# Feature-major token loads, centred on GpSimd, in place of sixteen TensorE transposes per sequence

## What is computed

```
x = x + attn(layernorm(x))            # linear attention without softmax
x = x + xattn(layernorm(x), ctx)      # cross-attention with softmax
x = x + ffn(layernorm(x))             # shared MLP plus 16 routed experts, top 2

attn, s = 4 heads of h = 128, xn = layernorm(x) as (b, t, a, e):
  Q    = einsum('btae,aeqf->qbtaf', xn, queries)
  pre  = einsum('qbtaf,buqf->qbtau', Q, xn)
  mix  = einsum('qbtau,buqg->abtqg', pre, xn)
  out  = einsum('abtk,akg->btag', mix, combiners)
```

## Time and profile before

| | |
|---|---|
| median of 3 runs | 1875.05 us (1871.57 to 1876.61) |
| the profiled execution: its time | 1873.81 us |
| the profiled execution: its span | 1872.1 us |
| TensorE busy | 1848.3 us (99%), mean granted clock 0.996 |
| VectorE, ScalarE, GpSimd busy | 821.4, 759.4, 837.7 us |
| 16 transposes of YT, per sequence | 1.75 us on TensorE |
| one round of phase 1 (Q end to Q end) | about 63 us |

### The profile page before, as it was taken

One profiled execution on the slowest core, in us unless ns is written; L12 is line 12 of the kernel. 1 busy time (PEld: TensorE's weight loads), 2 busy tenths in 40 slices (PEclk: granted clock), 3 DMA queues, 4 the chain that ended last, 5 costly groups with the idle time before them and its releaser, 6 DMA issues.

```text
span 1872.1 us, 27265 instructions
## 1 busy us (share of the span) xinstructions
PE 1848.3 (99%) x10224; PEld 1629.4 (87%) x10224; DVE 821.4 (44%) x2007; ACT 759.4 (41%) x1492; POOL 837.7 (45%) x727
## 2 busy tenths in 40 slices
PE   8999999999999999999999999999999999999997
PEld 6788888888878787888799999999999999999996
DVE  2575557555764434344332344323444234443332
ACT  3444444444454333333443444434444334444331
POOL 2132333233462423222555665656656666556631
PEclk9999999999999999999999999999999999999999
DMA  7002220221164333221767666766666666666732
GB/s 269 21 12 79 91 91 1 91 91 68 69 180 57 46 45 78 40 43 16 158 155 152 137 146 130 163 151 143 143 128 162 152 145 143 130 153 157 145 46 28
DMA packets 208498, 199.18 MB, mean 106 GB/s; under 512 B 132944, under 2 KB 132944, under 8 KB 208112
## 3 DMA queue, kind: packets, MB, share of 16 engines
q1 hardware_dynamic: 183072, 144.34, 29.2%
q0 software_dynamic: 25296, 53.11, 16.8%
HBM read 119.14 MB, written 48.91 MB: 90 GB/s over the span
## 4 chain that ended last, share of the span: by engine, by line
PE 96%; DVE 1%; ACT 1%; issue 1%; another core or an unknown queue 0%; DMA 0%; POOL 0%; SPq 0%; ACTq 0%; DVEq 0%; POOLq 0%
PE ps L71 63%; PE ps L1389 23%; PE ps L747 4%; PE ps L753 2%; PE ps L885 2%; PE ps L844 1%; PE ps L764 1%; DVE buffer L1291 0%; DVE buffer L1307 0%; ACT L1247 0%; ACT buffer L1247 0%; DMA buffer<-in_WkT 0%; ACT buffer L1205 0%; PE ps L823 0%
## 5 line engine op out<-in xcount | busy, mean ns | idle before, releaser
L71 PE MATMUL ps<-buffer,buffer 128*128 128x320 f32 (+1 forms) x6816 | 1224.1, 340 | 3.4 <-DVE buffer L648 2.1
L71 PEld LDWEIGHTS ps<-buffer,buffer 128*128 128x128 f32 x6816 | 1105.2, 188 | 109.7 <-issue 3.3
L1147 POOL TENSOR_TENSOR buffer<-buffer,buffer 128x512 fp32r<-128x512 f32 x289 | 379.5, 1478 | 247.4 <-ACT buffer L1205 247.0
L1389 PE MATMUL ps<-buffer,buffer 128*128 128x512 f32 x1904 | 437.7, 390 | 1.4 <-DVE buffer L1291 1.4
L1389 PEld LDWEIGHTS ps<-buffer,buffer 128*128 128x128 f32 x1904 | 355.9, 188 | 76.0 <-issue 2.0
L1205 ACT ACTIVATE buffer<-buffer 128x512 fp32r<-128x512 f32 (+1 forms) x491 | 293.6, 651 | 163.0 <-PE ps L1389 90.9
L1247 ACT ACTIVATE buffer<-ps 128x320 f32<-128x320 f32 (+1 forms) x240 | 112.4, 468 | 589.9 <-PE ps L71 563.8
L1307 DVE TENSOR_TENSOR ps<-ps,buffer 128x320 f32<-128x320 f32 (+2 forms) x198 | 100.2, 506 | 489.7 <-ACT buffer L1247 481.9
L1194 POOL DMA_INDIRECT out_tokens<-buffer,slot_list x80 | 125.9, 1573 | 185.5 <-DVE buffer L1337 179.8
L387 POOL DMA_INDIRECT slots<-pairs,slot_u x64 | 63.4, 991 | 189.1 <-DVE slot_u L734 171.9
L395 ACT ACTIVATE buffer<-ps 128x512 fp32r<-128x512 f32 (+1 forms) x180 | 97.2, 602 | 100.7 <-PE ps L71 40.0
(11 more groups left out here) (112 smaller groups left out, 1088.3 us busy)
## 6 DMA issues: line engine op xcount, KB each, us to landing
buffer<-in_wts SPq DMA_DIRECT2D x289, 256.0 KB
buffer<-in_x SPq DMA_DIRECT2D x8, 1024.0 KB, 6.5
buffer<-in_ctxT SPq DMA_DIRECT2D x8, 1024.0 KB, 7.9
out_tokens<-buffer SPq DMA_DIRECT2D x8, 1024.0 KB, 4.3
tokens_normed<-buffer SPq DMA_DIRECT2D x32, 256.0 KB, 3.2
out_tokens<-buffer POOLq DMA_DIRECT2D x32, 256.0 KB, 5.7
tokens_normed<-buffer POOLq DMA_DIRECT2D x1, 1280.0 KB, 11.8
out_tokens<-buffer POOLq DMA_DIRECT2D x1, 1280.0 KB, 13.9
```

What stands on the lines that cost most here:

```text
L71: last = pe.matmul(out, left, right, start=(c == 0 and i == 0), stop=(c == len(parts) - 1 and i == 2))
L1147: pool.tensor_tensor(wl[n % RING][:], wraw[n % RAW][:], wh[n % RING][:].bitcast(F32), ALU.subtract).then_inc(s_wl, 1)
L1389: ins = pe.matmul(down_bank[n % 2][:], left, right, start=(c == 0 and i == 0), stop=(c == FC - 1 and i == len(passes) - 1))
```

## The change

The host also passes the tokens with features on partitions (`xT`), which SyncE loads into the place of `yT`. After the statistics, VectorE copies the four means of each partition to a tile `mean` (L566 of the new file); SyncE stores it to a 512-number row in DRAM and loads that row back into `mean_row` on all 128 partitions (new step MEAN); GpSimd subtracts it from the four 128x512 blocks of `xT` in place. So A gets centred but unscaled tokens, and VectorE multiplies by `rstd` when it adds A to the tokens. The 16 transposes of YT and their four ScalarE copies are gone. The first of the four groups of SC now follows G directly on TensorE, ahead of T. At the start, QB comes ahead of T, and MEAN between C and WV. The core of the diff:

```diff
+    xT = at(8, [NC, S])
+    mean_row = at(42, [S])
-    yT = at(8, [NC, S])
...
+        def load_transposed(b):
+            sp.dma_start(xT[:], a["xT"][b].rearrange("(c p) n -> p c n", p=P)).then_inc(s_xT, 16)
+
+        load_transposed(0)
...
+            if name == "MEAN":
+                sp.wait_ge(s_mean, b + 1)
+                with nc.allow_non_contiguous_dma(reason="one number per partition and tile"):
+                    sp.dma_start(means[b].rearrange("(t p) -> p t", p=P), mean[:]).then_inc(s_mstored, 16)
+                sp.wait_ge(s_mstored, 16 * (b + 1))
+                if b >= 1:
+                    sp.wait_ge(s_centred, NC * b)
+                sp.dma_start(mean_row[:], means[b].partition_broadcast(P)).then_inc(s_mrow, 16)
+            if name == "A" and b + 1 < B:
+                filled(sp, "A", b, NT - 1)
+                load_transposed(b + 1)
...
+            if name == "MEAN":
+                pool.wait_ge(s_xT, 16 * (b + 1))
+                pool.wait_ge(s_mrow, 16 * (b + 1))
+                for c in range(NC):
+                    pool.tensor_tensor(xT[:, c, :], xT[:, c, :], mean_row[:], ALU.subtract).then_inc(s_centred, 1)
...
-                for c in range(NC):
-                    filled(act, "YT", b, c)
-                    bank = bank_of("YT", b, c)
-                    copy(yT[:, c, :], bank[:]).then_inc(s_ev["YT"], 1)
...
+            if k == 0:
+                dve.wait_ge(s_mstored, 16 * b)
+                dve.tensor_copy(mean[:], mv[:, :, 0]).then_inc(s_mean, 1)
...
-                    dve.tensor_tensor(x[b % XS][:, t, :], bank[:], x[b % XS][:, t, :], ALU.add).then_inc(s_ev["A"], 1)
+                    dve.scalar_tensor_tensor(x[b % XS][:, t, :], bank[:], rstd[0][:, t:t + 1], x[b % XS][:, t, :],
+                                             ALU.mult, ALU.add).then_inc(s_ev["A"], 1)
...
-                drained(pe, "Q", b - 1, 1)
-                if b == 0:
-                    drained(pe, "KR", 0)
-                    drained(pe, "W", 0, NC - 1)
-                for c in range(NC):
-                    transposes("YT", b, y, c)
+                if b >= 1:
+                    drained(pe, "Q", b - 1, NC - 1)
+                    scores(b - 1, 0)
...
-                drained(pe, "YT", b, NC - 1)
+                pe.wait_ge(s_centred, NC * (b + 1))
...
-                        last = pe.matmul(bank_of("A", b, t)[:, cols], yT[:, h, t * P:(t + 1) * P], M[:, cols],
+                        last = pe.matmul(bank_of("A", b, t)[:, cols], xT[:, h, t * P:(t + 1) * P], M[:, cols],
...
-                 ("T", i + 1), ("WV", i + 1), ("QB", i + 1), ("SC", i), ("M", i + 1), ("PT", i),
+                 ("MEAN", i + 1), ("QB", i + 1), ("T", i + 1), ("WV", i + 1), ("SC", i), ("M", i + 1), ("PT", i),
...
+            steps.remove(("MEAN", 0))
+            steps.insert(steps.index(("WV", 0)), ("MEAN", 0))
```

More of the change, by code:

```diff
@@ L78, in build @@
     slots = nc.dram_tensor("slots", (E * CAP, 2), F32, kind="Internal").ap()
+    means = nc.dram_tensor("means", (B, S), F32, kind="Internal").ap()
     with ExitStack() as ctx:
@@ L94, in build @@
             "slots": slots,
+            "means": means,
             "ps": [ctx.enter_context(nc.psum_tensor(f"ps{i}", [P, 512], F32)) for i in range(BANKS)],
@@ L103, in phase1 @@
     ident, slot_list, slots = shared["ident"], shared["slot_list"], shared["slots"]
+    means = shared["means"]
     ps = shared["ps"]
@@ L207, in phase1 @@
     mv = sb("mv", [P, NT, 2], F32)
+    mean = sb("mean", [P, NT], F32)
     veps, rt = sb("veps", [P, NT], F32), sb("rt", [P, NT], F32)
@@ L247, in phase1 @@
     s_dve = sem("s_dve")
+    s_mean, s_mstored, s_mrow = sem("s_mean"), sem("s_mstored"), sem("s_mrow")
+    s_xT, s_centred = sem("s_xT"), sem("s_centred")
     s_cnt = sem("s_cnt")
@@ L757, in tensor, with scores @@
         pe.wait_ge(s_const, 8)
+        def scores(b, t):
+            cols = slice(t * P, (t + 1) * P)
+            ready = (lambda c: drained(pe, "Q", b, c)) if (b, t) == (B - 1, 0) else None
+            three_pass(pe, bank_of("SC", b, t)[:], [(qh[:, c, cols], ql[:, c, cols], ch[:, c, :], cl[:, c, :])
+                                                    for c in range(NC)], ready).then_inc(s_mm["SC"], 1)
         def step(name, b):
@@ L772, in step @@
             if name == "QB":
-                drained(pe, "YT", 0, 0)
                 bank = bank_of("QB", b)
@@ L840, in step @@
                     pe.wait_ge(s_w, 32)
+                    drained(pe, "KR", 0)
+                    drained(pe, "W", 0, NC - 1)
                 drained(pe, "Q", b - 1, 3)
@@ L846, in step @@
             if name == "SC":
-                if b < B - 1:
-                    drained(pe, "Q", b, NC - 1)
-                else:
+                if b == B - 1:
                     drained(pe, "V", b, 1)
-                drained(pe, "YT", b + 1, 3)
-                for t in range(NT):
-                    cols = slice(t * P, (t + 1) * P)
-                    ready = (lambda c: drained(pe, "Q", b, c)) if (b, t) == (B - 1, 0) else None
-                    three_pass(pe, bank_of("SC", b, t)[:], [(qh[:, c, cols], ql[:, c, cols], ch[:, c, :], cl[:, c, :])
-                                                            for c in range(NC)], ready).then_inc(s_mm["SC"], 1)
+                for t in range(1 if b < B - 1 else 0, NT):
+                    scores(b, t)
             if name == "X":
@@ L1426 @@
         "x": np.asarray(x),
+        "xT": np.ascontiguousarray(np.asarray(x).transpose(0, 2, 1)),
         "ctxT": np.ascontiguousarray(np.asarray(ctx_1024).transpose(0, 2, 1)),
```

2 lines of the change are left out of this document (1 added, 1 removed).

## The result

The change makes the kernel **slower**: 1938.17 us (median of 4 runs, 1936.91 to 1939.71) against 1873.93 us for the kernel before (now the median of 4 runs; the 1875.05 ahead of the prediction was that of the first 3), a ratio of 1.0343 with a 95% interval of [1.033, 1.0356]. The profiled execution took 1936.91 us, its span is 1935.2, 63.1 more than the 1872.1 before. I had forecast 1870.8, a small gain, with a range from 1866.5 to 1878. The measured time is outside the range, and the change is a loss.

What follows compares the result with a forecast made beforehand. TensorE, busy 99% of the span, was taken as the bound. Transposes -12.25, rounds' chain 0, start +5.5 and clock +2.5 sum to -4.25 us: 1870.8 us against the 1875.05 median, range 1866.5 to 1878.

Steps and rivals of the forecast that it cites:

- the transposes: TensorE in rounds 0 to 6: YT's transposes removed, 1.75 us each round, -12.25 us in all.
- the chain of the means in the rounds: Statistics, store, row load and subtractions ahead of A: ready at 222.5, wanted at 223.8, so a term of 0.
- the start: A of sequence 0 waits for GpSimd's subtractions behind C: 5.5 us later, at 50.05; bounds 5.0 and 8.3.
- the clock at the start: TensorE idles about 7 us before A of sequence 0, which then runs at low clock, once: 2.5 us, bounds 0 and 4.
- The store of 512 numbers lands right behind it; I give it 0.5.: SyncE's queue in a round: the means' store lands 0.5 us after the 1 MB token load ahead of it.
- The 1.3 us of slack: Ahead of A in a round: centred tokens ready 1.3 us before TensorE wants them.
- The means come late: Rival: the small-piece store pays its own landing of 5.7, A waits 3.9 in five rounds, 1890.3 us; chance 0.11.
- Much of 5.7 is GpSimd's own issue: Argument against the late-means rival: much of the earlier small-piece store's 5.7 us landing was GpSimd issuing it.
- 5.4 when it is alone: The 1 MB token load ahead of the means' store in a round: lands after 5.4 us, 7.3 at most.
- The row load "2.7": Load of the means' row, 256 KB, in a round: 2.7 us, taken from stores of halves at 2.1 to 3.3.
- The row is there by 44: At the start: the means' row is loaded by 44 us, before GpSimd's step C ends.
- The extras of 0.5: At the start: C beginning up to 0.9 later and disturbed GpSimd subtractions, taken as 0.5 us in all.

Runs made afterwards that it cites:

- experiment 1: Kernel of the change with the means stored as 128 pieces of 16 bytes, GpSimd reading the row in that order: 1896.95 us, ratio 1.0124.
- experiment 7: Kernel of the change, start only: context load and sequence 0's means ahead of token loads 1 and 2, means subtracted before the zeros wait: 1928.87 us.
- experiments 5: Kernel of the change without store, row load or subtraction of the means, centring left out: 1865.68 us, ratio 0.9961 to the kernel before.
- 6: Kernel of the change without any means, centring left out, and with QB back behind WV: 1859.47 us, ratio 0.9922 to the kernel before.
- experiment 3: Kernel of the change with the means' store for sequences 2 to 7 issued earlier, at the head of PV: 1885.72 us, ratio 1.0047.
- 12: Sequence 0 as in the kernel before; sequences 1 to 7 by early 16-byte means stores, row load ahead of token load: 1861.24 us, ratio 0.9927.
- experiment 11: Kernel before plus only VectorE's copy of the means and the four-byte store behind the token load, nobody waiting: 1874.34 us, ratio 0.9995.
- experiments 10: Three kernels on experiment 3, centring left out: four-byte pieces 64 bytes apart, 16 bytes apart, or a quarter as many: 1872.07, 1871.32, 1878.2 us.
- experiment 4: Kernel of the change loading 128 different token rows instead of the means' row, centring left out: 1933.86 us (one execution).
- experiment 9: Kernel of the change with rearranged start, early store, 16-byte pieces, row load ahead of token load: 1868.24 us; with QB back behind WV: 1867.27 us.

## Why the prediction was wrong

Term by term, forecast and measured: the transposes -12.25 and -12.25; the chain of the means in the rounds 0 and 48.8 of waits, with another 10.1 of A at the low clock behind them; the start 5.5 and 13.4; the clock at the start 2.5 and 2.3, with 1.6 more in V and Q.

- **The step that failed** is this one: "The store of 512 numbers lands right behind it; I give it 0.5." The store took 11.7 us from issue in round 2, 6.25 more than in my chain. Together with the row load (5.5 instead of 2.7, and 0.1 to issue it), subtractions 0.1 shorter, and the store issued 1.1 us later against TensorE than I had it, that makes 22.3 - 13.2 + 1.1 = 10.2 us. The 1.3 us of slack are taken off: 8.9 us, and 8.98 were measured. The term of 0 became 48.8. Round 6 is in it with 5.4 us: I had counted it out because no token load stands in the queue there, but the store took 9.0 all the same.
- **Its rival was there, in kind.** *The means come late* named the small pieces as the cause, and experiment 1 bears it out. But I costed its strong form at 5.7 us from the earlier trace rows, which is a store of other pieces (40 bytes each), and from there argued down. "Much of 5.7 is GpSimd's own issue" was a wrong reading: the trace of before has 1.18 us for that issue. The same means in another layout take 1.4 us, and in the first one 8.1 to 13.6 in the rounds of all kernels that have it. A price that was in no row deserved a wide bound and more than 0.11. The row that I put next to it against the rival, "stores of 256 KB land after 2.1", is one of large pieces and says nothing of small ones.
- **The token load "5.4 when it is alone"**: with the store behind it, it landed after 9.7 to 12.4 in three of five rounds and after 5.4 and 5.5 in the other two. The wait in A was there in all five (7.8 to 9.1), so this is not what it came from.
- **The row load "2.7"** was taken from stores of the same size. To read one row 128 times took 4.4 to 7.5 us in the kernel of the change. Even with a store that lands as forecast (experiment 1) waits of up to 3.3 us are left, of which the row load has 2.4.
- **The clock, "due here, once"**: right in kind and in size at the start (A 6.10 instead of 3.84, 2.3 us; I had 2.5). But after each of the waits in the rounds the clock was at 0.50 too. I had priced a late chain as a wait alone, and never as a wait plus 1.5 to 2.0 us of A at the low clock (5.27 to 5.74 in TensorE's timeline, where it is 3.74 before). The shorter waits of experiment 1 brought it as well: A took 5.44 to 6.56 behind four waits of 2.5 to 3.3 us, and 3.81 behind one of 1.8.
- **The start**: A(0) at 57.94 instead of 50.05. "The row is there by 44" failed: it was there at 52.7, since the store took 23.9 and the load 7.5. The layout is part of this: with 16-byte pieces (experiment 1) the same store takes 19.1 and A(0) starts at 52.25. Even with the means early (experiment 7), a wait of 4.3 stayed. What I hadn't seen is that QB ahead of T moves VectorE's subtractions into GpSimd's, for 6.2 us once the means are out of the way (experiments 5 and 6). The extras of 0.5 were counted on GpSimd, and the loss is mainly on VectorE. In the kernel of the change itself this cost nothing: the zeros landed so late that VectorE's four were done, in 2.50 us, before step C began.
- **Right**: the transposes are worth 1.75 us each (rounds of 61.26, experiment 3; a ratio of 0.9922 for eight in 6, which is 14.6 us; 12.7 to 13.7 for seven in 12). The score group behind G waits for nothing, the scaled drain of A and the later context load cost nothing. (5.4 after 214.8 is 220.2 and not the 220.6 that I wrote; nothing hangs on it.) Of what I wrote as signs of a wrong forecast, the wait in A several times over came in all six rounds; the token load landing after 7 us came in three of five and not in each.

## What to carry to other kernels

When a value has to go through DRAM to change its layout, the form of the store decides: keep a partition's numbers together, or the small pieces apart (64 bytes here), and issue it one stage before it is needed: the slow store that nobody waited for cost nothing (experiment 11). Count what the new layout costs its reader, here 1.1 us of strided subtractions. A transfer for which no row exists gets its bounds from pieces of its own size and layout, and a wait on the bound engine costs its own length and the slow matmuls behind it. Where a step is expensive only in one place (here the start), keep the old way there and take the new one elsewhere.

## What the runs showed of the hardware

- Four-byte pieces that lie close together in DRAM are slow: 1.9, 2.3 to 3.0 and 8.7 to 11.5 us for 512 of them in the rounds, with one, four and sixteen to 64 bytes (experiments 10 and 3); 7.5 to 8.1 for 128 of them side by side. 128 pieces of 16 bytes, side by side, take 1.4.
- With such a store behind it in the same queue, a load of 1 MB was reported as landed after 10.2 to 11.6 us in three of five rounds, and after 5.5 and 5.7 in the other two (experiment 11).
- A load of one 2 KB row to 128 partitions takes 5.8 us (median of the kernel of the change), 128 different rows 3.7 us (experiment 4).
- GpSimd's four 128x512 subtractions take 4.93 us, and 6.0 when one input is read with a stride of four numbers (experiment 1).
- VectorE instructions with two SBUF inputs beside GpSimd's: one took 11.2 us instead of 0.68, while GpSimd's own four went from 4.93 to 6.29 at most (experiment 7), and the strided four from 6.0 to 6.91 (experiment 9). The Trainium skill, GPSIMD Engine Reference, section Key points, says that GpSimd shares its SBUF interfaces with VectorE and contends with VectorE's instructions that have two SBUF inputs; the rows agree, and show VectorE as the one that is held up most.
- TensorE's clock: in round 2 the engine stands from 248.7 us and the row from 254 us has 0.50. In each of the six rounds with a wait (5.4 to 9.1 us) A took 5.27 to 5.74 us instead of 3.74.
